# Filler mask products, the second pair's query projection and the order of the last down products in an attention and mixture-of-experts kernel

## The reference

```python
x = x + xattn(layernorm(x), ctx, ctx)      # 16 heads of 16, rotary q and k
    # row s of a sequence attends to rows s-64 .. s of the context
    # softmax(q k / 4) v, then the output projection and its bias
x = x + ffn(layernorm(x))                  # 8 experts, top 2
    # logits = xf @ router_w.T ; p = softmax(logits) ; top 2, normalised
    # for each expert e: mask = rows that chose e
    #   mean_w = mean of the weights of those rows for e
    #   out += mask * ((silu(xf @ gate_w[e].T) * (xf @ up_w[e].T)) @ down_w[e].T) * mean_w
```

## Time and profile before

| | |
|---|---|
| median of 3 runs | 479.04 us (479.0 to 481.38) |
| the profiled execution, its time | 480.83 us |
| its span, first to last instruction | 479.0 us |
| mean granted TensorE clock | 0.974 |
| PE busy | 450.5 us, 94% of the span |
| DVE busy | 302.7 us, 63% |
| ACT busy | 274.3 us, 57% |
| POOL busy | 141.7 us, 30% |
| chain that ended last | PE 72%, DVE 7%, ACT 6%, issue 5%, DMA 4%, POOL 3% |

### The profile page before, as it was taken

One profiled execution on the slowest core, in us unless ns is written; L12 is line 12 of the kernel. 1 busy time (PEld: TensorE's weight loads), 2 busy tenths in 40 slices (PEclk: granted clock), 3 DMA queues, 4 the chain that ended last, 5 costly groups with the idle time before them and its releaser, 6 DMA issues.

```text
span 479.0 us, 9047 instructions
## 1 busy us (share of the span) xinstructions
PE 450.5 (94%) x2816; PEld 368.7 (77%) x2816; DVE 302.7 (63%) x742; ACT 274.3 (57%) x866; POOL 141.7 (30%) x174
## 2 busy tenths in 40 slices
PE   7899999999999999899999999999999999999980
PEld 4556675757566655478999999999999999999980
DVE  3846969798989878765647646366475573763320
ACT  2458787888887878325455446364454554554230
POOL 5201014453627253662032050140500503205013
PEclk9979999999999999979999999999999999999995
DMA  5640082020202021239856645565464544213002
GB/s 179 207 103 3 15 295 90 25 68 7 66 8 63 11 60 36 74 92 374 300 159 154 208 76 154 154 131 173 105 178 134 104 156 98 26 38 41 1 3 35
DMA packets 24332, 50.38 MB, mean 105 GB/s; under 512 B 5282, under 2 KB 15046, under 8 KB 24138
## 3 DMA queue, kind: packets, MB, share of 16 engines
q10 hardware_dynamic: 6480, 22.55, 15.0%
q1 hardware_dynamic: 11658, 20.26, 13.6%
q0 software_dynamic: 6144, 6.97, 8.8%
HBM read 39.62 MB, written 13.20 MB: 110 GB/s over the span
## 4 chain that ended last, share of the span: by engine, by line
PE 72%; DVE 7%; ACT 6%; issue 5%; DMA 4%; POOL 3%; POOLq 0%; SPq 0%; ACTq 0%; DVEq 0%
PE b_o L735 9%; PE b_small L735 9%; PE b_s L722 7%; PE b_s L724 7%; PE b_s L723 7%; PE b_s L462 6%; ACT probs L857 4%; PE b_pv L485 4%; PE b_proj L515 3%; PE b_pt L471 3%; PE b_s L460 3%; PE b_proj L541 3%; PE b_pt L722 2%; PE b_pt L724 2%; PE b_pt L723 2%
## 5 line engine op out<-in xcount | busy, mean ns | idle before, releaser
L857 ACT ACTIVATE probs<-b_s,negmax 100x100 f32<-100x100 f32 x256 | 85.4, 357 | 19.0 <-DVE negmax L1152 12.4
L1368 POOL DMA_INDIRECT out<-y_sb,idnow x32 | 49.7, 1552 | 156.8 <-ACT y_sb L900 149.4
L888 ACT CAST h_hi<-h_sb 128x448 fp32r<-128x448 f32 x64 | 36.3, 567 | 87.1 <-DVE h_sb L1232 87.1
L722 PE MATMUL b_s<-x_hi,w_hi 128*128 128x448 f32 x192 | 71.0, 370 | 1.0 <-DVE h_sb L1232 0.9
L724 PE MATMUL b_s<-x_hi,w_lo 128*128 128x448 f32 x192 | 69.8, 363 | 0.0
L723 PE MATMUL b_s<-x_lo,w_hi 128*128 128x448 f32 x192 | 69.3, 361 | 0.0
L1129 DVE TENSOR_TENSOR w_lo<-w_raw,w_hi 128x1024 fp32r<-128x1024 f32 x48 | 58.8, 1224 | 13.8 <-ACT w_hi L822 13.4
L1236 DVE TENSOR_TENSOR h_lo<-h_sb,h_hi 128x448 fp32r<-128x448 f32 x64 | 40.0, 625 | 40.6 <-ACT h_hi L888 39.9
L857 ACT ACTIVATION_READ_ACCUMULATOR probs<-b_s,negmax 100x1 f32 x256 | 55.7, 218 | 0.0
L462 PE MATMUL b_s<-kblk,qrot 128*100 128x400 f32 x128 | 54.3, 505 | 0.0
L1152 DVE TENSOR_REDUCE negmax<-b_s 100x4 f32<-100x400 f32 x64 | 36.2, 566 | 24.2 <-PE b_s L462 23.9
(11 more groups left out here) (158 smaller groups left out, 979.9 us busy)
## 6 DMA issues: line engine op xcount, KB each, us to landing
w_raw<-in_ffw ACTq DMA_DIRECT2D x42, 512.0 KB, 3.9
xin<-slots SPq DMA_DIRECT2D x10, 449.8 KB, 4.5
slots<-in_padrows SPq DMA_DIRECT2D x9, 449.8 KB, 4.1
w_raw<-in_ffw SPq DMA_DIRECT2D x6, 512.0 KB, 8.2
kblk<-krot SPq DMA_DIRECT2D x120, 12.5 KB
out<-x_all SPq DMA_DIRECT2D x8, 200.0 KB
ctx_all<-in_ctxT SPq DMA_DIRECT2D x1, 1200.0 KB, 6.5
x_all<-in_x SPq DMA_DIRECT2D x1, 1200.0 KB
```

Of the source, the lines that this page charges most:

```text
L722: pe.matmul(o, wh[:, c, cols], x_hi[:, c, :], start=(c == 0), stop=False)
L857: m = nc.scalar.activation(probs[:, N % 3, h, :], b_s[N % 3][0:S, h * S:(h + 1) * S], ACT.Exp, bias=negmax[:, N % 4, h:h + 1], accum_out=p ...
L888: nc.scalar.copy(h_hi[:, f, :], h_sb[:, f % 2, :]).then_inc(s_hhi, 1)
L1368: G.indirect_dma_start(out, bass.IndirectOffsetOnAxis(idnow[:, n:n + 1], 0), y_sb[:, n, :], None, bounds_check=TOK + TILE - 1, oob_is_err= ...
```

## The change

Three places are touched.

- **Fillers.** In the last two rounds `warm(3)` becomes `warm(5)` in slot 5 of round 8, `warm(3)` becomes `warm(8)` and `warm(2)` becomes `warm(4)` in slot 0 of round 9, and a new `warm(4)` stands behind `late_rows(6)` in slot 2 of round 9.
- **Second pair's query projection.** In round 0 alone, `q_project(1)` moves from slot 3 to slot 4 on PE, the queries' evacuation on ACT from slot 2 to slot 3, and `k_rotate(1)` on DVE from slot 2 to slot 3.
- **Last down products.** The last three slices are computed for row groups 0 and 1 first and then for groups 2 and 3, where group 2 had come with the first two. `take_output` scales one row group of 256 columns at a time, four instead of two activations, and POOL waits for each row group by itself. The semaphore `s_y` counts to four per tile in place of two, with two more initial credits.

```diff
--- before.py
+++ after.py
@@ -161,7 +161,7 @@
         dest = sb("dest", [S, TOPK * 2])
         desti = sb("desti", [S, 2, TOPK * 2], U32)
         wacc = sb("wacc", [S, E])
-        credit = sb("credit", [1, 4])
+        credit = sb("credit", [1, 2 + GRP])
         table = sb("table", [1, 1])
 
         cnt = sb("cnt", [P, E])
@@ -646,18 +646,18 @@
                     if n == 5 and i == NPAIR:
                         warm(5)
                         early_tile()
-                        warm(3)
+                        warm(5)
                     if n == 5 and 0 <= i - 2 < NPAIR:
                         ranks(i - 2)
                     if n == 2 and prv:
                         den_transpose(2 * i - 1)
                     if n == 0 and i == NPAIR + 1:
-                        warm(3)
+                        warm(8)
                     if n == 0 and 0 <= i - 2 < NPAIR:
                         x2_transpose(i - 2)
                     if n == 0 and i == NPAIR + 1:
-                        warm(2)
-                    if n == 3 and nxt:
+                        warm(4)
+                    if n == (4 if i == 0 else 3) and nxt:
                         if i < 0:
                             idle(2)
                         q_project(i + 1)
@@ -727,7 +728,7 @@
             def project_down(par, t, f, groups=range(GRP)):
                 pe.wait_ge(s_hlo, FC * t + f + 1)
                 if f == 0:
-                    pe.wait_ge(s_y, 2 * t + 2)
+                    pe.wait_ge(s_y, GRP * t + GRP)
                 wh, wl = wpart(w_hi[par])[2], wpart(w_lo[par])[2]
                 for g in groups:
                     o = b_y[g // 2][0:ROWS, g % 2 * D:(g % 2 + 1) * D]
@@ -749,10 +750,10 @@
                     if f >= 3:
                         project_down(par, t, f - 3)
                 for f in range(FC - 3, FC - 1):
-                    project_down(par, t, f, range(3))
+                    project_down(par, t, f, range(2))
                 project_down(par, t, FC - 1, range(2))
                 for f in range(FC - 3, FC - 1):
-                    project_down(par, t, f, (3,))
+                    project_down(par, t, f, range(2, GRP))
                 project_down(par, t, FC - 1, range(2, GRP))
                 if last:
                     tile_transpose(t + 1)
@@ -869,7 +870,7 @@
                         nc.scalar.copy(ident_bf[:, :], cst[:, C_ID:C_ID + P]).then_inc(s_setup, 1)
                         nc.scalar.copy(mask_bf[:, :, :], cst[:, C_MASK:C_MASK + S].unsqueeze(1)
                                        .to_broadcast([P, QH, S])).then_inc(s_setup, 1)
-                    if n == 2 and nxt:
+                    if n == (3 if i == 0 else 2) and nxt:
                         evac_proj(i + 1, 0, s_q, s_qc)
 
 
@@ -895,11 +896,11 @@
             def take_output(t, e):
                 a.wait_ge(s_idnow, t + 1)
                 a.wait_ge(s_mean, 1)
-                for n in range(GRP // 2):
-                    a.wait_ge(s_down, 2 * t + n + 1)
-                    nc.scalar.activation(y_sb[:, 2 * n:2 * n + 2, :].rearrange("p g d -> p (g d)"),
-                                         b_y[n][0:ROWS, :], ACT.Copy, scale=meanw[0:ROWS, e:e + 1]
-                                         ).then_inc(s_y, 1)
+                for n in range(GRP):
+                    if n % 2 == 0:
+                        a.wait_ge(s_down, 2 * t + n // 2 + 1)
+                    nc.scalar.activation(y_sb[:, n, :], b_y[n // 2][0:ROWS, n % 2 * D:(n % 2 + 1) * D],
+                                         ACT.Copy, scale=meanw[0:ROWS, e:e + 1]).then_inc(s_y, 1)
 
             def step(t, e, par, split, again):
 
@@ -1129,7 +1130,7 @@
                 V.tensor_tensor(w_lo[1 - par][:, cols], w_raw[:, cols], w_hi[1 - par][:, cols],
                                 ALU.subtract).then_inc(s_wlo, 1)
 
-            for n, free in enumerate((s_xt[DC - 1], s_id, s_y, s_y)):
+            for n, free in enumerate((s_xt[DC - 1], s_id) + (s_y,) * GRP):
                 V.memset(credit[:, n:n + 1], 0.0).then_inc(free, 1)
             xn_stats(0)
             xn_write(0)
@@ -1172,7 +1173,7 @@
                         rows_low(NPAIR - 1)
                     if n == 2 and prv:
                         attend(2 * i - 1)
-                    if n == 2 and nxt and i >= 0:
+                    if n == (3 if i == 0 else 2) and nxt and i >= 0:
                         k_rotate(i + 1)
                     if n == 2 and 0 <= i - 2 < NPAIR:
                         choose(i - 2)
@@ -1353,7 +1354,7 @@
             total = g.value_load(first[0:1, E:E + 1], min_val=1, max_val=MAXTILES)
             with g.Fori(0, total) as t:
                 taken, added = g.to_reg(t + 2), g.to_reg(16 * GRP * (t + 1))
-                copied, halves = g.to_reg(t + 1), [g.to_reg(2 * t + 3 + n) for n in range(2)]
+                copied, groups = g.to_reg(t + 1), [g.to_reg(GRP * (t + 1) + 1 + n) for n in range(GRP)]
 
 
                 g.wait_ge(s_first, 1)
@@ -1362,9 +1363,8 @@
                 g.wait_ge(s_first, 1)
                 g.wait_ge(s_idnow, copied)
                 for n in range(GRP):
-                    if n % 2 == 0:
-                        g.wait_ge(s_first, 1)
-                        g.wait_ge(s_y, halves[n // 2])
+                    g.wait_ge(s_first, 1)
+                    g.wait_ge(s_y, groups[n])
                     G.indirect_dma_start(out, bass.IndirectOffsetOnAxis(idnow[:, n:n + 1], 0), y_sb[:, n, :], None,
                                          bounds_check=TOK + TILE - 1, oob_is_err=True,
                                          compute_op=ALU.add).then_inc(s_add, 16)
```

## The result

The changed kernel took 477.19 us (median of 16 runs, 475.71 to 480.85) against 480.27 us for the kernel before (16 runs beside it, 477.19 to 482.89). The ratio is 0.995, with a 95% interval of 0.993 to 0.997: faster, by 3.1 us in the medians and 2.4 us by the ratio, where 6.2 were forecast, and outside the range of 471.3 to 475.9. The profiled execution took 480.72 us, one of the two slowest of the sixteen, with a span of 478.6 us.

A forecast was written before the change was run, and what follows sets the result against it. PE sets the time nearly everywhere, leaving two slow-clock stretches, the idle time ahead of them and the tail; 3.9 + 1.4 + 0.9 = 6.2 us off, a predicted median of 472.8 us, range 471.3 to 475.9.

The forecast's parts named there:

- Part 1: Round 0, second pair's query projection: moving it removes PE's idle time and the slow clock, 3.9 us, bounds 0 and 4.7.
- if the clock then holds, so does the loss in the slow stretch: Round 0 from 24.4 to 31.0 us: with the lull filled, 6.12 us of half-clock work would gain 3.06 us.
- The 0.7 us for `values(3)` behind ACT: Round 0: `values(3)` waits until about 30 us for ACT's later work, PE reaching it at about 29.3; 0.7 us lost.
- rival E: Round 1, slot 2: pair 1's key blocks land late, PE stands and the clock falls; slower, 482 us; chance 0.03.
- B: Round 0: the clock falls all the same at about 24.4 us, 1.35 in place of 3.9 won, 475.4 us; chance 0.10.
- Part 2: Rounds 8 and 9: fillers keep the clock up, `x_hi` comes 1.8 us earlier, of which 1.4 us is counted.
- Rival C: Round 9: the clock falls all the same and new fillers run at half clock; 3.6 us off, 475.4 us; chance 0.10.
- Does the first tile keep it?: First expert tile: its end moves only as scatter and `xin` load do; between 0.55 and 1.8 us, 1.4 us taken.
- the 0.55 us of the lower bound: First tile: POOL's last four scatters began after 0.85 us waiting for DVE, of which 0.55 us can go.
- If the scatter waits for them to drain: First tile: weight reloads begin 1.8 us earlier, so a scatter waiting for the DMA engines lands 1.8 us earlier; upper bound.
- Rival D: First tile: the clock holds but the tile waits for `xin` as before; 5.2 us off, 473.8 us; chance 0.13.
- Part 3: End of the last tile: reordered down products and shorter scaling move the four last DMAs 0.9 us earlier, bounds 0.2 and 0.95.

The follow-up runs named there:

- after: First profile of the whole changed kernel: the profiled execution took 480.72 us with a span of 478.6 us.
- e1: Kernel before with only the second pair's query projection moved in round 0: 477.26 us, ratio 0.9953 to the kernel before.
- e2: Kernel before with only the 13 fillers added: 478.95 us, ratio 0.9991 to the kernel before.
- e3: Kernel before with only the new order of the last down products and scaling by row group: 479.25 us, ratio 0.9992 to the kernel before.
- e4: The whole change, unedited, beside its three parts alone: 476.28 us, ratio 0.9931 to the kernel before.
- e5: Kernel before without an edit, for a second profile: 477.95 us with a span of 476.1 us.
- e6: Kernel before with weight reloads of the second and third expert cut to an eighth of their columns: 481.24 us, ratio 1.0015 to the kernel before.
- e7: Changed kernel with the second and third experts' weight reloads cut to an eighth: 473.29 us, ratio 0.9859 to the kernel before.
- e8: Fillers alone with the second and third experts' weight reloads cut to an eighth: 475.80 us, ratio 0.9898 to the kernel before.
- e12: Kernel before without an edit, for a third profile: 481.36 us with a span of 479.5 us.
- e13: The whole change, unedited, beside the late-reload runs on one chip: 476.51 us, ratio 0.9932 to the kernel before.
- e14: Changed kernel with the third expert's weight reloads one slice later, repeated beside the unedited change: 476.45 us, ratio 0.9926 to the kernel before.
- e15: Kernel before with the third expert's weight reloads one slice later: 480.02 us, ratio 0.9997 to the kernel before.
- e16: Fillers alone with the third expert's weight reloads one slice later: 477.73 us, ratio 0.9972 to the kernel before.
- e18: The whole change, unedited, in the last series: 475.24 us, ratio 0.9923 to the kernel before.
- e9: Changed kernel with the third expert's padding rows written one expert later: 475.29 us, ratio 0.9903 to the kernel before.
- e10: Changed kernel with the third expert's weight reloads one slice later: 474.22 us, ratio 0.9881 to the kernel before.
- e11: Changed kernel with both later padding rows and the third expert's reloads one slice later: 474.50 us, ratio 0.9869 to the kernel before.
- e17: Changed kernel with the first tile's own load cut to the last 16 numbers of each row: 475.10 us, ratio 0.9923 to the kernel before.
- light kernels: Kernels before, changed and with fillers alone, each with two experts' weight reloads cut to an eighth: 481.24, 473.29 and 475.80 us.

## Why the prediction was right in direction and wrong in size

The stages of all twenty profiles, in us, explain it. "Projection" runs from the first scores product to round 0's `v_project`, "rows" from the last but one pair's transposes to the last pair's (rounds 8 to 9), "x_hi" from there to the first tile's `x_hi`, "tile" from there to the second tile's.

| profile | projection | rows | x_hi | tile |
|---|---|---|---|---|
| predicted from | 19.24 | 11.40 | 9.12 | 30.84 |
| after | 14.79 | 11.35 | 7.51 | 34.86 |
| e1 | 14.79 | 11.34 | 9.11 | 30.87 |
| e2 | 17.82 | 11.34 | 7.58 | 31.45 |
| e3 | 17.92 | 12.13 | 9.11 | 33.16 |
| e4 | 14.79 | 11.34 | 7.55 | 31.54 |
| e5 (before) | 16.40 | 12.21 | 7.54 | 31.41 |
| e6 (light) | 17.82 | 12.21 | 7.94 | 30.86 |
| e7 (light) | 14.80 | 11.35 | 7.60 | 29.23 |
| e8 (light) | 17.84 | 11.34 | 7.53 | 29.25 |
| e12 (before) | 17.91 | 11.97 | 9.11 | 31.98 |
| e13 | 14.79 | 11.40 | 7.52 | 30.87 |
| e14 | 14.80 | 11.41 | 7.55 | 34.44 |
| e15 | 16.41 | 12.26 | 7.77 | 31.27 |
| e16 | 16.41 | 11.36 | 7.52 | 31.00 |
| e18 | 14.79 | 11.34 | 7.60 | 31.35 |

(e9, e10, e11 and e17 have 14.79 or 14.80, 11.33 to 11.35, 7.55 to 7.60, and tiles of 31.32, 29.63, 32.93 and 31.59.)

**Part 1: the mechanism held, its main term was mis-sized.** This is the failed step that is shown best. It is "if the clock then holds, so does the loss in the slow stretch, 6.12 us of work at half clock, 3.06 us". The clock does hold, in each of the eleven profiles with this part. But without it the stage took 19.24 us in one of nine profiles, the one predicted from, 17.82 to 17.92 in five, and 16.40 or 16.41 in three, where the lull of 1.65 us stands and the clock does not fall. With the part it is 14.79 us in all eleven, so the gain is 4.45, about 3.05 or 1.6 us, (4.45 + 5 x 3.05 + 3 x 1.6) / 9 = 2.7 us on average, in line with the 2.25 us of e1. The 0.7 us for `values(3)` behind ACT did not come: 4.45 is within 0.3 us of the full 4.7. The key blocks' DMAs began 9.53 us after the first scores in place of 8.68, 0.85 us later (1.0 was forecast), and no profile has PE waiting for them; rival E did not happen, nor did B. The transposes in the filled gap did no harm, some 8 to 14 of the 40 products there: in e1 and e18 the stretch from 24.4 us has 6.27 and 6.28 of 6.60 us busy at 1.00. The rule that the prediction took from the Trainium skill ("TensorE: Matmul & The Clock Gate", Part 4, PE-mode transpose), that transposes don't count as PE-busy as products do, would, as the prediction read it, have had the clock fall here; with this mixture of both, the traces don't show it.

**Part 2: right at `x_hi`, too high behind it, its worth in the whole not settled.** The prediction had 1.8 us at `x_hi`. With the fillers it starts 7.51 to 7.60 us after the last transposes in all thirteen profiles, against 9.11 or 9.12 in the four where the clock fell 3 to 5 us after the transposes: 1.55 us. In e6 and e15 it fell 7 us after them, and `x_hi` came at 7.94 and 7.77. The prediction saw one fall and none from 191 to 200 us; five of the seven profiles without fillers have one there, 0.6 to 0.9 us in the column "rows", and those without fillers have at least one of the two. So the fillers win more than was seen, 1.6 us on average from the last but one pair's transposes to `x_hi`: 19.75 to 21.24 us (mean 20.5) without, 18.85 to 18.96 with. Rival C did not happen.

The step that failed is "Does the first tile keep it?", with 1.4 us: the runs of e2 give 0.4 us, those of the whole change less part 1 and part 3 about as much, e16 more. Already the tile's first product, which the prediction also had 1.4 us nearer, comes 9.69 us after the transposes in after and e4, in place of 10.36: 0.7 us, and 1.1 us in e2 and e18. PE stands there 0.6 us for POOL's `wacc` in after and e4.

Behind it, POOL's last scatter begins 15.2 to 15.9 us after the last pair's transposes whatever the clock of PE does, 15.81 in the profile predicted from, so the 0.55 us of the lower bound are there in some executions and not in others; `x_hi` comes earlier and the scatter does not. "If the scatter waits for them to drain" did not hold: the weights are asked for earlier, and the scatter still lands 6.60 (e4, by its chain of waits), 7.20 (after) and 7.32 us (e17) after its issue, 6.27 us before.

In the profiles of the whole change where the tile runs well (e4, e13, e18) and in e2, 49.8 to 50.4 us lie between the last but one pair's transposes and the second tile's `x_hi`; before it was 51.36, and 51.16 in e5. That is 0.9 to 1.6 us against the execution predicted from. In two profiles, after and e14, the second tile's transposes begin 7.3 us after the issue of their load, in place of 4.2 to 5.1 us in those just named; PE stands for 1.8 to 2.2 us, then the clock falls, and the tile is 3 us longer. e11 lost 1.5 us with a wait of 1.8 us for DVE and a fall behind it. No profile without the fillers has such a fall behind a wait (e3 lost some 2 us there in another way, below).

Over all profiles with the full loads this stretch took 51.2 to 54.4 us (mean 52.1) in the six without the fillers and 48.5 to 53.7 us (mean 50.8) in the eleven with them. That is 1.3 us of the 1.6, but with a spread wider than the difference. The light kernels show that the load has a part in it: with it the fillers are worth 0.4 us (e2, its interval from 1.7 faster to 0.8 slower), without it 5.4 us. How much of the 1.4 us it takes in a usual execution is not shown. Rival D, the tile bound by its loads, has 0.4 us in its sum for this part, which is what e2 gave.

**Part 3: right, with a small cost missed.** 0.9 us was forecast; from the last tile's `x_hi` to the last add are 39.53 or 39.54 us with it and 40.41 or 40.42 without. The two pieces of 256 columns take 0.84 us, 0.85 by the forecast. Not foreseen: a middle tile takes 0.03 us longer (156.39 to 156.41 us for five with this part, 156.22 to 156.24 without), about 0.2 us over all. The net of 0.65 us is inside the interval of e3.

**From the execution to the median.** e4 and e18 have a span of 472.8 us, which is the figure that the sum gave. That is in part luck: in e4 the projection gave 4.45 us in place of 3.9, and `x_hi` and the tile together 0.9 us in place of 1.4. The rest of the error is the last step, "The median of the runs shown is 479.04 ... so I predict 472.8 us". It took the whole loss of the profiled execution off a median in which that loss is mostly smaller, and the median of three, 479.04, became 480.27 with sixteen. The changed kernel's own executions beside it reach from 475.71 to 480.85 us; the fastest of them lies at the upper end of the range. The profile after is 5.8 us longer than that of e4: its first scores came 2.3 us later, behind the fall at 12 us, and its first tile took 3.3 us more.

**What stays open.** Why the same lull brings a long, a short or no fall of the clock. What the fillers are worth with the full loads, 0.4 us by e2 and more by e16. Which transfers hold the scatter and the two loads: later padding rows and a later reload were not shown to help, a smaller first load left the time as it was, and the reloads of the second expert's weights, cut only together with the third's, were not tried alone. The clock's fall at 12 us in the profile of after is there in e11 too, where the first scores came at 17.72 us (18.50 in after, 16.12 to 16.97 in the other eighteen); it was not followed up.

## What to carry to other kernels

A fall of the clock behind a lull can be in one execution and not in the next: take two or three profiles of the kernel before, price the fall by their mean and not by the one at hand, and look in the windows for falls that the page's tenths hide. Where a stage behind the gain starts with transfers in a row, work out what dates them; if another engine or the DMA load does, part of the gain may end there. Compare a candidate with the version that it should beat, side by side: e10's edit had a ratio of 0.9881 to the kernel before, and 0.9926 in e14, with 0.9932 for the unedited version beside it.

## What the hardware showed that was not expected

- The same eight products behind the same lull of 1.65 us took 2.74 to 3.04 us in six executions and 1.62 us in three, in programs equal up to there.
- A transfer of 28 KB, in pieces of 64 bytes, landed 4.13 us after its issue, one of 450 KB after 4.31 to 7.33 us in the same place of other executions; in the light kernels one of 450 KB landed after 3.31 to 3.65 us. A sixteenth of the bytes did not bring the landing below that.
- Issuing three reloads of 512 KB took ACT's queue 1.71 us in the kernel before and 4.33 us in e3, and the first `silu` of that tile began 8.60 us after `x_hi` in place of 5.39 (7.43 in e12). Why is not known. The timeline of ACT in e3:

```profile
214.05 4.33 ACTq L892 DMA_DIRECT2D w_raw<-in_ffw  x3
219.63 0.54 ACT L884 ACTIVATE act<-b_s 128x448 f32<-128x448 f32 x1 [5.80 <-issue]
```
